# Expert results of a mixture-of-experts stage: added on chip to rows fetched from the output, in place of a scatter-add into an accumulator that is copied out

## What is computed

```python
x = x + _L3_xattn_ref(_layernorm(x), ctx_2048, mask_BxS2_bk0)
x = x + _L3_ffn_ref(_layernorm(x), gate_w, w1, w2, w3)

# _L3_ffn_ref: T = 2048 rows, E = 8 experts of 896 hidden units, top 2
probs = softmax(x @ gate_w.T)
top_w, top_i = top_k(probs, 2)
top_w = top_w / sum(top_w)
w_dense = zeros((T, E)).at[arange(T)[:, None], top_i].add(top_w)
for e in range(E):
    h = silu(x @ w1[e].T) * (x @ w3[e].T)
    out = out + w_dense[:, e:e + 1] * (h @ w2[e].T)
```

## Time and profile before

| what | us |
|---|---|
| median of 3 runs (lowest, highest) | 2321.14 (2319.14, 2321.93) |
| the profiled execution | 2322.72 |
| its span | 2320.9 |
| TensorE busy (PE, modelled) | 2065.3 (89%) |
| VectorE busy (DVE) | 1601.7 (69%) |
| ScalarE busy (ACT) | 1237.4 (53%) |
| GpSimd busy (POOL) | 302.0 (13%) |
| mean granted clock of TensorE | 0.947 of full |

### The profile page before, as it was taken

One profiled execution on the slowest core, in us unless ns is written; L12 is line 12 of the kernel. 1 busy time (PEld: TensorE's weight loads), 2 busy tenths in 40 slices (PEclk: granted clock), 3 DMA queues, 4 the chain that ended last, 5 costly groups with the idle time before them and its releaser, 6 DMA issues. The chain is left out here.

```text
span 2320.9 us, 46693 instructions
## 1 busy us (share of the span) xinstructions
PE 2065.3 (89%) x18816; PEld 1575.8 (68%) x18816; DVE 1601.7 (69%) x2974; ACT 1237.4 (53%) x2455; POOL 302.0 (13%) x307
## 2 busy tenths in 40 slices
PE   7978989899899898888879898979889879999996
PEld 4644458677555787556657666758656658999996
DVE  5756657676465897777858877857566676766763
ACT  2325664544466444555546456565478524665663
POOL 0010000011310000001000000000100113444432
PEclk9978999899999999899989999999899879999998
DMA  3020010100100002000020000010200035666663
GB/s 120 22 66 23 14 44 1 37 1 1 60 20 24 12 1 72 1 1 1 1 78 10 9 18 0 0 37 1 73 2 2 7 120 184 207 193 221 197 206 89
DMA packets 62793, 126.10 MB, mean 54 GB/s; under 512 B 16073, under 2 KB 45386, under 8 KB 62442
## 3 DMA queue, kind: packets, MB, share of 16 engines
q1 hardware_dynamic: 53770, 111.35, 14.3%
q0 software_dynamic: 8832, 12.06, 2.6%
HBM read 109.18 MB, written 15.80 MB: 54 GB/s over the span
## 5 line engine op out<-in xcount | busy, mean ns | idle before, releaser
L268 PE MATMUL ps<-ffn_xh,ffn_wh 128*128 128x256 f32 x644 | 184.0, 286 | 1.5 <-DVE ffn_xl L4379 1.5
L268 PE MATMUL ps<-ffn_xh,ffn_wl 128*128 128x256 f32 x644 | 182.4, 283 | 0.0
L268 PE MATMUL ps<-ffn_xl,ffn_wh 128*128 128x256 f32 x644 | 182.3, 283 | 0.0
L4374 DVE TENSOR_TENSOR ffn_wl<-ffn_fresh,ffn_wh 128x1792 fp32r<-128x1792 f32 x69 | 139.5, 2024 | 26.4 <-ACT ffn_wh L4254 26.4
L216 POOL TENSOR_TENSOR all_rstd<-all_mv,all_cst 128x4 f32<-128x4 f32 x40 | 8.4, 210 | 1063.6 <-DVE all_mv L194 1063.6
L1981 DVE SCALAR_TENSOR_TENSOR attn_xc<-attn_cx,all_w,attn_xc 128x512 f32<-128x512 f32 (+1 forms) x144 | 107.3, 749 | 48.2 <-ACT attn_xc L1832 44.7
L268 PEld LDWEIGHTS ps<-ffn_xh,ffn_wh 128*128 128x128 f32 x644 | 123.5, 192 | 1.7 <-DVE ffn_xl L4379 1.7
L4254 ACT ACTIVATE ffn_wh<-ffn_fresh 128x1792 fp32r<-128x1792 f32 x69 | 117.0, 1695 | 14.4 <-DMA ffn_fresh<-in_l3f_w 14.4
L268 PEld LDWEIGHTS ps<-ffn_xl,ffn_wh 128*128 128x128 f32 x644 | 123.4, 192 | 0.0
L268 PEld LDWEIGHTS ps<-ffn_xh,ffn_wl 128*128 128x128 f32 x644 | 123.4, 192 | 0.0
L3028 ACT ACTIVATE xattn_sc<-xattn_sc,xattn_mx 128x128 f32<-128x128 f32 x256 | 98.8, 392 | 17.7 <-DVE xattn_mx L3126 17.7
(11 more groups left out here) (483 smaller groups left out, 6079.4 us busy)
## 6 DMA issues: line engine op xcount, KB each, us to landing
ffn_fresh<-in_l3f_w SPq DMA_DIRECT2D x69, 896.0 KB, 4.9
all_w<-in_ctxT SPq DMA_DIRECT2D x12, 512.0 KB, 5.7
all_w<-in_ctx SPq DMA_DIRECT2D x8, 512.0 KB, 6.7
all_x<-in_x_rows SPq DMA_DIRECT2D x4, 512.0 KB, 7.3
all_x<-x_seq SPq DMA_DIRECT2D x4, 512.0 KB, 5.4
all_w<-in_l2x_o SPq DMA_DIRECT2D x1, 2048.0 KB, 9.3
all_w<-in_l2f_up SPq DMA_DIRECT2D x1, 2048.0 KB, 8.4
xattn_ctxT<-in_ctxT SPq DMA_DIRECT2D x4, 512.0 KB, 3.7
```

The source lines that it names most:

```text
L268: last = pe.matmul(out, a, b, start=start and n == 0, stop=stop and n == 2)
L4374: dve.tensor_tensor(wl[:, j % 2, piece(q)], fresh[:, piece(q)], wh[:, j % 2, piece(q)].bitcast(F32), ALU.subtract).then_inc(low_ready.sem, 1)
```

## The change

The accumulator `x_acc` and the last copy are gone. phase_xattn3 stores x into the output itself. In phase_ffn3, GpSimd fetches the two tiles of rows of block j from the output into `y[j % 2]` (`fetch`, an indirect DMA each), VectorE adds the expert's result times its share in one operation (`add`, in place of ScalarE's `outputs`), and GpSimd stores the rows back with an indirect DMA that doesn't accumulate (`store`). fetch(j) waits until every store of block j - 1 has landed, a store for its add and for the store before. The output has no rows to spare for unused slots: their numbers lie beyond its end, and the DMAs skip them by a bounds check. y is cleared once at the start.

```diff
@@ phase_xattn3
-    acc, rows = k.x_acc, k.xn_rows
+    acc, rows = k.out_rows, k.xn_rows
...
-            sp.dma_start(acc[ROWS:ROWS + P, :], zeros[:, :]).then_inc(rows_stored.sem, 16)
...
-            sp.wait_ge(*rows_stored(0, 32 + 32 * GROUPS))
+            sp.wait_ge(*rows_stored(0, 16 + 32 * GROUPS))
@@ phase_ffn3, GpSimd
+            def target(at):
+                return bass.IndirectOffsetOnAxis(ap=row_i[:, at:at + 1], axis=0)
+
+            def fetch(j):
+                if j >= 1:
+                    pool.wait_ge(*stored(0, 16 * SLOT_TILES * j))
+                for v in range(SLOT_TILES):
+                    pool.indirect_dma_start(y[:, j % 2, v, :], None, acc[:, :], target(SLOT_TILES * j + v),
+                                            bounds_check=ROWS - 1, oob_is_err=False).then_inc(fetched[v].sem, 16)
+
+            def store(j, v):
+                at = SLOT_TILES * j + v
+                pool.wait_ge(*y_ready(0, at + 1))
+                if at >= 1:
+                    pool.wait_ge(*stored(0, 16 * at))
+                pool.indirect_dma_start(acc[:, :], target(at), y[:, j % 2, v, :], None,
+                                        bounds_check=ROWS - 1, oob_is_err=False).then_inc(stored.sem, 16)
+
+            pool.wait_ge(*y_clear(0, 1))
             pool.wait_ge(*lists_ready(0, 1))
             gather(0)
             gather(1)
             for j in range(BLOCKS):
                 if j + 2 < BLOCKS:
                     gather(j + 2)
+                fetch(j)
                 for v in range(SLOT_TILES):
-                    at = SLOT_TILES * j + v
-                    pool.wait_ge(*y_ready(0, at + 1))
-                    if at >= 1:
-                        pool.wait_ge(*added(0, 16 * at))
-                    pool.indirect_dma_start(acc[:, :], bass.IndirectOffsetOnAxis(ap=row_i[:, at:at + 1], axis=0),
-                                            y[:, j % 2, v, :], None, compute_op=ALU.add).then_inc(added.sem, 16)
-            pool.wait_ge(*added(0, 32 * BLOCKS))
+                    store(j, v)
+            pool.wait_ge(*stored(0, 16 * TILES))
@@ phase_ffn3, ScalarE
-            def outputs(j, v):
-                act.wait_ge(*out_psum(0, SLOT_TILES * j + v + 1))
-                if v == 0 and j >= 2:
-                    act.wait_ge(*added(0, 32 * (j - 1)))
-                at = SLOT_TILES * j + v
-                act.activation(y[:, j % 2, v, :], O[v][:, 0:D], ACT.Copy,
-                               scale=share[:, at:at + 1]).then_inc(y_ready.sem, 1)
...
-                    if u == 1 and j >= 1:
-                        outputs(j - 1, 0)
...
-                    if u == 2 and j >= 1:
-                        outputs(j - 1, 1)
...
-            for v in range(SLOT_TILES):
-                outputs(BLOCKS - 1, v)
@@ phase_ffn3, VectorE
+            dve.memset(y[:, :, :, :], 0.0).then_inc(y_clear.sem, 1)
...
+            def add(j, v):
+                at = SLOT_TILES * j + v
+                dve.wait_ge(*out_psum(0, at + 1))
+                dve.wait_ge(*fetched[v](0, 16 * (j + 1)))
+                dve.scalar_tensor_tensor(y[:, j % 2, v, :], O[v][:, 0:D], share[:, at:at + 1], y[:, j % 2, v, :],
+                                         ALU.mult, ALU.add).then_inc(y_ready.sem, 1)
...
                     product(n)
                     if n >= 1:
                         low(n - 1)
+                    if u == 2 and j >= 1:
+                        add(j - 1, 0)
+                    if u == 3 and j >= 1:
+                        add(j - 1, 1)
                     if u == 1 and j + 1 < BLOCKS:
                         inputs(j + 1)
                     if u < PIECES and j + 1 < BLOCKS:
                         split(j + 1, u)
             low(U * BLOCKS - 1)
+            for v in range(SLOT_TILES):
+                add(BLOCKS - 1, v)
@@ build
-        k.x_acc = nc.dram_tensor("x_acc", (ROWS + P, D), F32, kind="Internal").ap()
+        k.out_rows = out.rearrange("b p d -> (b p) d")
...
-        with nc.Block() as block:
-            @block.sync
-            def _(sp):
-                sp.dma_start(out.rearrange("b p d -> b (p d)").rearrange("b (q n) -> (b q) n", q=8),
-                             k.x_acc[0:ROWS, :].rearrange("(a r) d -> a (r d)", r=P // 8)).then_inc(x_out.sem, 16)
-                sp.wait_ge(*x_out(0, 16))
```

More of the change, by code:

```diff
@@ L4189, in phase_ffn3 @@
     y_ready = Signal(k, "y_ready")
-    added = Signal(k, "added")
+    fetched = [Signal(k, f"fetched{v}") for v in range(SLOT_TILES)]
+    stored = Signal(k, "stored")
+    y_clear = Signal(k, "y_clear")
     def piece(q):
@@ L4544, in build @@
         k.x_back = Signal(k, "x_back")
-        x_out = Signal(k, "x_out")
         k.nf4 = Nf4(k, k.arena(0))
@@ L4575, in build @@
                 make(k, k.arena(n), (loads[n].sem, 16 * counts[n]), load_next(n + 1))
-        k.phase, k.phase_ctx = "all", ctx
-        with nc.Block() as block:
-            @block.sync
-            def _(sp):
-                sp.dma_start(out.rearrange("b p d -> b (p d)").rearrange("b (q n) -> (b q) n", q=8),
-                             k.x_acc[0:ROWS, :].rearrange("(a r) d -> a (r d)", r=P // 8)).then_inc(x_out.sem, 16)
-                sp.wait_ge(*x_out(0, 16))
 def kernel(**inputs):
```

## The result

| | before | changed |
|---|---|---|
| median (lowest to highest), us | 2320.2 (2319.1 to 2321.9) | 2407.4 (2402.2 to 2411.2) |
| ratio, 95% interval | | 1.0375 (1.0359 to 1.0391) |
| span of the profiled execution | 2320.9 | 2409.4 |

The change costs 87 us, 3.75%. The forecast said slower, 2372 us, and the time lies inside its range of 2328 to 2420; the size is 35 us too small.

What follows compares the result with a forecast made beforehand. Blocks of 16.01 us were taken as bound by the TensorE, ScalarE, VectorE chain, TensorE nearly full. Loop +52.0, adds in other blocks +1.0, memset +1.0, tail -3.0: +51 on 2321.1 gives 2372, range 2328 to 2420.

Steps and rivals of the forecast that it cites:

- The slack of the gathers: In ffn3, gathered rows land 2.6 us ahead of TensorE's turn to them; the change spends this.
- The loop: ffn3 block: turn, add, store, landing, second store, gathers, landing, turn; 18.3 us, 18.6 with half clock, +52.0 over 20 blocks.
- the heavier rival: In ffn3 weights hold the first store until 13.2; with half clock every other block 21.5 us, +110, 2430; chance 0.15.
- the term of 3.9 us for the first store's landing: In ffn3's loop, the store issued at 6.8 lands 3.9 us later, at 10.7, in an opening between weight pieces.
- the long end: ffn3 loop with long landings (6.0 for the store, 6.5 for the gather) and long issues: 24.8 us a block, +176.
- the half clock's share: TensorE idling before turns brings 1.2 GHz, up to 1.6 us a loop; one block in five, 0.3 a block.
- Adds: Two VectorE operations a block in ffn3, 0.40 us each; delay TensorE 0.6 at most, 0.4 taken, block 16.4 by this alone.
- Fetches: GpSimd's fetches of output rows for the next block's adds in ffn3 cost zero, hidden by the gather's own lateness.
- Tail: End of ffn3: copy and its step, 14.2 us, go, but a chain of last stores and fetch replaces them: -3.0.
- one of the signs: In the profile after, the last landing comes 16 to 18 us after TensorE's end.
- gathers on time: Stores in ffn3 land after some 2.3 us, blocks stay at 16.4, time 2328; chance 0.13.
- faster: Stores land within 2.3 us, adds hide in VectorE's shadow, blocks stay at 16.0: -8, 2313; chance 0.06.

Runs made afterwards that it cites:

- adds_early_only: Kernel before the change, with VectorE instead of ScalarE taking a block's two results out of PSUM, still in units 1 and 2: 2365.5 us, ratio 1.0200.
- Thin weights: Changed kernel loading only 8 of 128 partitions of the weights of blocks 2 to 22: 2361.9 us, ratio 1.0183.
- adds_only: Kernel before the change, with VectorE instead of ScalarE taking a block's two results out of PSUM, in units 2 and 3: 2442.5 us, ratio 1.0515.
- direct: Kernel before the change, its accumulating scatter aimed at the output with a bounds check, and no copy at the end: 2308.6 us, ratio 0.9950.
- ahead_unchained: Changed kernel with gathers issued a block earlier, ahead of the stores, and no wait between a block's two stores: 2324.1 us, ratio 1.0017.
- no_fetch: Changed kernel with the fetches of blocks 1 to 22 left out: 2407.4 us, ratio 1.0383.
- gather_ahead: Changed kernel with a block's two gathers issued one block earlier, ahead of the two stores: 2367.8 us, ratio 1.0205.
- early_adds: Changed kernel with VectorE's two adds one unit earlier, in units 1 and 2: 2355.6 us, ratio 1.0154.

## Why the prediction was right, and where its size came from

**The bound before, and what was spent.** Right. The slack of the gathers was the thing to watch: adds_early_only spends just that and goes to 18.2 us a block. Its size, 2.6, was read from one block, whose second gather landed after 4.2; I called that usual, but over the blocks from 1960 to 2220 the second gather lands after 4.2 to 5.5, 4.7 in the mean, and the slack is nearer 2.

**The loop, step by step**, counted from the turn at 2103.04 (the landing of the second gather, and with it the next turn, closes it):

| step | predicted | measured |
|---|---|---|
| first add starts | 6.0 | 6.3 |
| first store starts | 6.8 | 7.6 |
| it has landed | 10.7 | 14.0 |
| second store starts | 11.4 | 14.9 |
| second gather starts | 14.6 | 17.5 |
| it has landed, turn | 18.3 | 20.3 |

The order of events, the engines and the wait at the end are as predicted. The block of 20.55 us lies above the 17.4 to 20 of the forecast itself; that the time is inside the stated range is owed to the range's upper part, which took in half of the heavier rival. **The step that failed is the term of 3.9 us for the first store's landing.** It measured 6.4. The reasoning was that a store issued at 6.8 would come out in the same opening as a scatter that was issued at 4.5, at 10.6 to 10.8; no such opening shows. The store left 0.8 later than assumed, between two pieces of the weights, and landed behind the second. The row that I had at the long end, 6.0, was the better estimate. Thin weights put 2.7 us of the 6.4 down to the weights, and 1.0 is the store's issue, 2.0 us long beside VectorE's piece.

All terms of the loop in order, which lead from the predicted 18.3 to the measured 20.3: +0.3 until the add, the half clock's share (the prediction had set 0.3 a block aside for it beside the 18.3); +0.5 from the add's end to GpSimd's start, 0.77 of issue with a bounds check, where adds_only without one shows 0.27, on the same engine and behind the same add. I had bounded the check's cost by 0.6 either way and taken 0; direct, before's kernel with the check, shows 0.72. +2.5 landing; +0.2 from the landing to the second store; -0.6 for shorter issues (1.0 for the plain second store, not 1.6); -0.9 for the gathers' landing, 2.7 rather than 3.6. Sum +2.0. In the mean over 20 blocks it was 20.55 against 18.6, 39 us. With a start 2.7 us later and a tail 2.9 us better than forecast this is again 39, for a profiled execution that ran 4 us above the median; of the median 35 us were missed. (Two small slips in the sums carry no weight: three blocks at 0.4 are 1.2 and not 1.0, and 6.8 + 6.5 is 13.3 and not 13.2.)

**Adds.** Length 0.477 us, spacing 0.40, as predicted. Their price where nothing else binds is 0.6 us a block (ahead_unchained), the most that was given for it and 0.2 over what was taken; in the changed kernel itself TensorE's wait for the gathers hid them, but for the 0.4 of the first one that the loop passes through. The memset of y took 0.91 us, where 1.0 was predicted.

**Fetches.** Zero, right (no_fetch); in the 20 blocks no add of the changed kernel waited for one. In gather_ahead and early_adds, where the gathers are earlier, adds do wait for them, by 35 and 58 us in total.

**Tail.** -3.0 predicted, -5.9 measured. The chain of stores, fetch, add and stores is there, and starts 1.6 us later behind the last turn than forecast, but each landing was shorter than the 3.7 taken from the accumulating form:
```profile
2391.75 2.15 DMA out_x<-ffn_y,ffn_row_i
...
2394.78 2.12 DMA out_x<-ffn_y,ffn_row_i
...
2397.72 2.13 DMA ffn_y<-out_x,ffn_row_i
```
The last store lands some 10 us behind TensorE's last matmul (2406.4 against 2396.3), and not 16 to 18, which was one of the signs. By the fixed part and the bytes that the Trainium skill (DMA: Bandwidth & Descriptors, "Anatomy of one DMA") gives, 2.3 us is an estimate for such a transfer, and these quiet rows agree with it within 0.2. In the loop, under weights, the same store measured 6.4, so that the rivals "gathers on time" and "faster", which rested on 2.3 us there, did not come.

**The clock.** Right in kind, and near in size. In each of 20 blocks TensorE waited ahead of the turn, 3.2 us in the mean. In 2 us behind the turn (from 0.7 on) the granted clock was below full in 15 of 19 blocks and 1.00 in the other 4. Stretches of the changed kernel (us of the stretch, busy us of PE, PEld, DVE, ACT and POOL, PEclk, DMA share, GB/s), behind the turns at 1999.81, 2103.04 and 2265.80:
```profile
2000.51:2002.51 2.00, 2.00 (x19) 2.00 (x18) 0.69 (x1) 2.00 (x2) 0.58 (x1) 1.00 0.08 15
...
2104.00:2106.00 2.00, 2.00 (x12) 2.00 (x11) 0.74 (x2) 1.92 (x2) 0.62 (x1) 0.50 0.38 108
...
2108.00:2109.50 1.50, 1.50 (x15) 1.50 (x14) 1.35 (x3) 1.43 (x3) 0.00 (x0) 1.00 0.49 76
...
2266.50:2268.50 2.00, 2.00 (x11) 2.00 (x11) 0.69 (x1) 1.55 (x2) 1.50 (x2) 0.50 0.13 32
```
0.50 is the 1.2 GHz level. The Trainium skill (TensorE: Matmul & The Clock Gate, "Why this matters for your kernels") has the half clock come back after a gap between bursts, and that agrees with 15 of the 19 blocks; in the other 4 the clock stayed full behind the gap. The cost depends on how long it stays low. In 11 of the 15 the first add starts 6.3 us behind the turn, and these blocks take 20.3 us in the mean, no more than the 20.4 of the four at full clock. In the other 4, among them the one at 2265.80, the add starts at 7.2 to 7.3 and the block takes 21.3. So the half clock came far more often than in one block in five, but cost a whole microsecond only in about one in five, some 0.2 a block in the mean, close to the 0.3 that the prediction set aside.

**The rivals.** "Heavier" had the first store held by the weights, out at 13.2; measured 14.0. What kept the time under its 2430 are the second half of the loop, 6.3 us where this rival had 7.5, and the clock's small share. The change came out between the forecast and this rival.

## What to carry to other kernels

On an engine that issues its DMAs in order, ask not only what a new transfer costs but what stands behind it: prefetches queued behind a store inherit the store's data, its wait and its landing, and a landing under other traffic was three times the quiet one here. Before work moves to another engine, compare the time at which each engine comes to it; 74 to 77 us here hung on one unit of place and 44 to 47 on the engine, with the work itself worth 12. And take the parts of a change singly: the copy was worth 13 us by itself, and could be had by aiming the accumulation at the output.

## What was not expected of the hardware

- The same indirect store of 128 rows of 1 KB landed after 2.1 us in the quiet tail and after up to 6.9 in the loop, counted from the start of its issue, with 4.4 the median of all that the profile lists:
```profile
DMA to landing us min/median/max: 2.1/4.4/6.9
```
- Its issue on GpSimd took 1.0 us, but 2.0 where it ran beside VectorE's 2 us subtraction of a weight piece (2110.67 beside 2109.75 to 2111.77); the accumulating form took 1.55 and 3.1 in the same two settings.
- A bounds check adds about 0.45 to 0.5 us ahead of an indirect DMA that had to wait for an engine's result (0.27 without, 0.72 to 0.77 with it). It lies in the path of the data each time.
- In the tail of direct an accumulating scatter landed after 2.7 us, where before it took 3.7. Target, bounds check and skipped slots all differ between the two, and which of them does it stays open.
